# GpSimd's weight splitting placed behind the first layernorm's operations, two per-row scalars, and the dummy matmuls of the steady state taken out

## What is computed

```
x = x + linear_attention(layernorm(x))         # 16 heads of 16, feature elu(.)+1, own wq wk wv wo and biases
x = x + cross_attention(layernorm(x), ctx)     # 16 query heads, 4 key/value heads, ALiBi bias, mask, softmax
x = x + moe(layernorm(x))                      # 8 experts of 176, top 2, plus a shared expert of 352
layernorm(x) = (x - mean) / sqrt(var + 1e-5)
```

## Time and profile before

| | |
|---|---|
| three runs | 467.52, 468.42, 465.21 us; median 467.52 |
| profiled execution | 467.31 us, span of its instructions 465.5 us |
| mean granted TensorE clock | 0.957 |
| busy PE, DVE, ACT, POOL | 393.8, 299.8, 222.8, 216.4 us |
| attention pipeline | to about 270 us, the expert stage to 465.5 us |

### The profile page before, as it was taken

The page is one execution under the profiler, slowest core; times in us unless marked ns, Lnnn a source line. Parts: engine busy times, 40 slices in busy tenths (PEclk is TensorE's granted clock), DMA queues, the critical chain, the costliest instruction groups (busy, mean ns, idle before and its releaser), DMA issues.

```text
span 465.5 us, 12494 instructions
## 1 busy us (share of the span) xinstructions
PE 393.8 (85%) x4014; PEld 329.3 (71%) x4014; DVE 299.8 (64%) x808; ACT 222.8 (48%) x576; POOL 216.4 (46%) x252
## 2 busy tenths in 40 slices
PE   7888899888988899889997868999999999998300
PEld 5666667666776667667776757999988999887200
DVE  2636877778667877788764268666666566655166
ACT  2224356544664356544544274788445555544200
POOL 1135567565766567665554200777214444333300
PEclk9989999999999999999999997999999999999755
DMA  7910213151141420500000000223323333332396
GB/s 183 328 64 13 57 46 104 56 147 46 18 140 55 129 58 14 145 11 0 13 1 2 2 0 1 103 102 107 97 59 115 114 114 114 113 95 89 98 283 218
DMA packets 30583, 40.21 MB, mean 86 GB/s; under 512 B 6354, under 2 KB 23634, under 8 KB 30546
## 3 DMA queue, kind: packets, MB, share of 16 engines
q1 hardware_dynamic: 24210, 27.56, 20.9%
q0 software_dynamic: 3456, 9.46, 5.7%
q10 hardware_dynamic: 2880, 2.69, 1.8%
HBM read 22.88 MB, written 16.81 MB: 85 GB/s over the span
## 4 chain that ended last, share of the span: by engine, by line
PE 52%; DVE 18%; issue 12%; DMA 7%; ACT 2%; POOL 2%; DVEq 1%; POOLq 0%; SPq 0%; ACTq 0%
PE ps L761 22%; PE ps L524 5%; DVE smax L1252 4%; PE ps L640 4%; DMA y_rows<-e_y,out_row 4%; PE ps L627 3%; DMA yg<-y_rows 3%; PE ps L602 3%; PE ps L533 2%; PE ps L571 2%; PE ps L856 2%; DVE xn L1239 2%; PE ps L841 2%; DVE kv_bd L1202 1%; PE ps L515 1%
## 5 line engine op out<-in xcount | busy, mean ns | idle before, releaser
L495 POOL DMA_INDIRECT y_rows<-e_y,out_row x40 | 38.4, 959 | 69.6 <-ACT e_y L1110 32.7
L761 PE MATMUL ps<-w_hi,xh 128*128 (+1 forms) x144 | 49.8, 346 | 9.4 <-DVE xl L1363 5.8
L436 POOL TENSOR_TENSOR sc<-sc,smax 128x1024 f32<-128x1024 f32 x16 | 32.7, 2041 | 43.3 <-DVE smax L1252 43.3
L761 PE MATMUL ps<-w_hi,xl 128*128 (+1 forms) x144 | 47.3, 328 | 0.0
L761 PE MATMUL ps<-w_lo,xh 128*128 (+1 forms) x144 | 47.0, 327 | 0.0
L487 POOL DMA_INDIRECT xs_rows<-x_send,pos x32 | 30.9, 966 | 29.8 <-DVE pos L1462 20.4
L681 PE MATMUL ps<-zeros 128*128 128x256 f32 x142 | 40.2, 416 | 4.2 <-DVE key_off L1297 2.9
L429 POOL TENSOR_TENSOR bias_t<-alibi,key_off 128x1024 f32<-128x1024 f32 x16 | 37.8, 2364 | 0.0
L761 PEld LDWEIGHTS ps<-w_hi,xh 128*128 128x128 f32 x144 | 27.4, 190 | 13.6 <-issue 6.4
L402 POOL TENSOR_TENSOR st<-mv,eps 128x1 f32<-128x1 f32 x32 | 6.1, 190 | 59.9 <-DVE mv L1164 30.7
L681 PEld LDWEIGHTS ps<-zeros 128*128 128x128 f32 x142 | 26.4, 201 | 7.9 <-issue 3.1
(11 more groups left out here) (178 smaller groups left out, 1143.8 us busy)
## 6 DMA issues: line engine op xcount, KB each, us to landing
w_stage<-in_w_ffn_dram SPq DMA_DIRECT2D x12, 496.0 KB, 3.8
xs_rows<-zeros SPq DMA_DIRECT2D x5, 1028.0 KB, 7.3
xs<-xs_rows SPq DMA_DIRECT2D x40, 128.5 KB, 2.1
yg<-y_rows SPq DMA_DIRECT2D x16, 256.0 KB, 3.8
ctxT<-in_ctxT_dram SPq DMA_DIRECT2D x16, 128.0 KB, 2.1
out_dram<-y ACTq DMA_DIRECT2D x16, 128.0 KB, 3.8
x_all<-in_x_dram SPq DMA_DIRECT2D x1, 1664.0 KB, 9.8
y_rows<-e_y,out_row POOLq DMA_INDIRECT x40, 2.9
```

Source lines behind the costliest of these rows:

```text
L436: nc.gpsimd.tensor_tensor(v, v, spread(smax[:, :].rearrange("p (h o) -> p h o", o=1), 2, S), ALU.subtract).then_inc(sm["sub_ready"], 1)
L495: nc.gpsimd.indirect_dma_start(out=y_d[:, :], out_offset=bass.IndirectOffsetOnAxis(ap=out_row[:, q:q + 1], axis=0), in_=e_y[:, q, :], in_o ...
L761: mm = T.matmul(out_ap, lhs, rhs[rows, cols], start=st, stop=en)
```

## The change

Three edits. On POOL `rstd1(t+2)` is issued before `split_low` and no longer behind it. On DVE `xn1` and `xn2` are tensor_scalars: one tensor, and two scalars per row. On PE the two zero matmuls in `transpose_x2` (t = 0 to 14) and the single one in `transpose_o2` (tiles 0 to 13) are gone; the other dummy matmuls stay.

```diff
                 if has(t, 0):
                     rstd2(t)
+                if has(t, 2):
+                    rstd1(t + 2)
                 if splits(t):
                     split_low(t - FIRST_SPLIT, q)
-                if has(t, 2):
-                    rstd1(t + 2)
...
             def transpose_x2(t):
                 pe.wait_ge(sm["q1_ready"], 2 * (t + 2 if has(t, 1) else t + 1))
-                if has(t, 1):
-                    keep_warm(A0, 2)
                 pe.wait_ge(sm["ln2_done"], t + 1)
...
             def transpose_o2(t):
-                if has(t, 2):
-                    T.matmul(ps[:, B0, 2 * P:4 * P], zeros[:, 0:P], zeros[:, 0:D], start=True, stop=True)
                 pe.wait_ge(sm["o2_ready"], t + 1)
...
             def ln1_norm(t):
-                V.scalar_tensor_tensor(out=xn1[:, :], in0=xt(t), scalar=mv1[:, 0:1], in1=spread(rs1[:, :], 1, D),
-                                       op0=ALU.subtract, op1=ALU.mult).then_inc(sm["ln1_done"], 1)
+                V.tensor_scalar(xn1[:, :], xt(t), mv1[:, 0:1], rs1[:, :], ALU.subtract, ALU.mult).then_inc(sm["ln1_done"], 1)
...
             def ln2_norm(t):
-                V.scalar_tensor_tensor(out=xn2[:, :], in0=xt(t), scalar=mv2[:, 0:1], in1=spread(rs2[:, :], 1, D),
-                                       op0=ALU.subtract, op1=ALU.mult).then_inc(sm["ln2_done"], 1)
+                V.tensor_scalar(xn2[:, :], xt(t), mv2[:, 0:1], rs2[:, :], ALU.subtract, ALU.mult).then_inc(sm["ln2_done"], 1)
```

## The result

The changed kernel takes 445.11 us, the median of four runs (442.98, 446.16, 447.91, 444.06). The kernel before took 467.97 us beside it (four runs, 465.21 to 469.15). The ratio is 0.9523 with a 95% interval of 0.9451 to 0.9595, so it is faster by 4.8%. The forecast was 441.5 us in a range of 437.5 to 449.5. The profiled execution is the fastest of the four: 442.98 us, 24.3 us under the profiled 467.31 of before.

What follows compares the result with a forecast made beforehand. It took a 15.01 us loop through PE and DVE, with xn2 stalled by POOL's split, as the bound: 467.31 - 23.2 - 2.8 - 0.7 + 0.6 = 441.2, plus 0.3 for the clock, gives 441.5 us. Range 437.5 to 449.5.

Steps and rivals of the forecast that it cites:

- Exclusion of DVE and POOL: In the loop, a DVE operation with two SBUF inputs waits for a running POOL operation; xn2 took 2.40 us for 0.48.
- doesn't do it: Rival: xn2 stalls for another reason than POOL's split, so the time stays at 464 to 468 us; chance 0.02.
- The split behind `rstd1`: On POOL in t = 2 to 13: moving the split removes xn2's stall, 1.93 us an iteration, 23.2 us over twelve.
- The collision with `xn1`: On DVE, xn1 meets the last 0.10 us of the moved split; 0.05 us an iteration, 0.6 us in all.
- Two per-row scalars: On DVE, xn1 and xn2 take 0.36 us each, saving 0.12 each time: 2.8 us in the loop, 0.7 before it.
- The clock at the start: In t = 0 and 1, fewer PE records before gaps could bring a second low-clock stretch: 0.3 us, ends 0 and 1.5.
- The dummies: PE's zero matmuls cost nothing before the change; kept after it, the pair would hide 1.1 us of gain each time.
- PE's own loop: PE's iteration without its waits and the zero matmuls: 12.54 us, 0.30 under the new loop of 12.84.
- PE becomes the bound: Rival: PE or a hidden chain sets the loop, costing 0.3 to 1.0 us an iteration, 445 to 454 us; chance 0.15.
- POOL's subtraction goes first: Rival: the split ends late and xn1 waits for all of subtract_max, 2.07 us an iteration, 465 us; chance 0.06.
- The clock falls in the loop: Rival: without dummies PE loses full clock, 8.8 us per wholly low iteration, 494 us with six; chance 0.03.

Runs made afterwards that it cites:

- order_back: The kernel after with POOL's split ahead of rstd1 again, scalars per row and no dummies kept: 486.36 us for 483.49 before, ratio 1.0065.
- split_later: The kernel after with an unused POOL addition of zeros ahead of the split, so that it ends later: 469.22 us for 483.33 before, ratio 0.9724.
- order_only: The kernel before with only rstd1 moved ahead of the split on POOL: 444.13 us for 466.13 before, ratio 0.9522.
- dummies_back: The kernel after with all the removed dummy matmuls put back: 461.50 us for 483.49 before, ratio 0.9535.
- warm_start: The kernel after with a pair of zero products ahead of transpose_x2 in t = 0 and 1 only: 456.43 us for 483.49 before, ratio 0.9429.
- no_dummies_only: The kernel before with only the dummy matmuls taken out: 489.12 us for 483.33 before, ratio 1.0119.
- stt_back: The kernel after with the old two-tensor form of xn1 and xn2: 461.53 us for 483.49 before, ratio 0.9526.
- warm_gaps: The kernel after with zero products: a pair in t = 0 and 1, six at the start of t = 1, three behind its transpose_x2; ratios 0.9428 and 0.9419.

## Why the prediction was right, and where its steps were not

The sign, the mechanism and the range were right: 445.11 lies in 437.5 to 449.5. It is 3.6 us above the 441.5. The profiled execution is only 1.5 us above it, and that is in part luck, as the last sum shows. Step by step:

1. **Exclusion of DVE and POOL: right.** `xn2` took 2.28 to 2.43 us in the twelve iterations and takes 0.40, and came back to 2.25 when only the order was undone (`order_back`). The change that "doesn't do it" is excluded. The prediction left open whether the new form is held too: it is.

2. **The split behind `rstd1`: right in place and size.** Start 0.91 us after the score addition (0.90 predicted), end 3.21 after it (3.19). The stall of 1.93 us an iteration is gone. The collision with `xn1` was booked at 0.05 us and costs nothing: a held tensor_scalar ends 0.15 us after POOL's operation, which is 185.50 us here, and `xn1` ends at 185.63 anyway. A longer collision costs, as the 0.43 us of `split_later` show (122.98 for 122.55). The weight loads, started later, stay hidden: ACT's `split_high` waits for nothing in the loop.

3. **Two per-row scalars: right in kind, too large.** The estimate was 0.36 us, from the 0.29 of L1339 and 0.07 for a scalar; it is 0.40, with 0.31 or 0.32 to the next start in place of 0.27. An operation saves 0.07 us and not 0.12. The loop by the measured terms is 15.01 - 2.00 (stall and `xn2`, 2.32 to 0.32) - 0.07 (`xn1`) = 12.94 us, for 12.95 in the trace and 12.84 forecast. Over twelve iterations that is 1.3 us of the error. Before t = 2 the 0.7 us booked were too much as well: `order_only` and `dummies_back` differ by this edit alone, and take 15.43 and 15.29 us in t = 0, 12.67 and 12.53 in t = 1, so 0.28 us of it are shown.

4. **The clock at the start: the term of the sum that was mis-sized most.** I booked 0.3 us within ends of 0 and 1.5, from the earlier trace rows. Measured were +2.19 us in t = 1 of the profiled execution, outside those ends, and 0.87 and 0.93 in two others. I had seen the danger ("four records less before such gaps in t = 0 and 1") and priced it by one short operation, L588. But the low stretch lasts from 39 to 45 us and takes in `project_q2` and all that follows it. `warm_start` shows the cause: two pairs of zeros put back in t = 0 and 1 bring t = 1 to 12.53 us.

5. **The dummies: "cost nothing as the kernel stands" held for the waits, not for the clock.** PE did idle behind them. But they also held the clock under the stall: `no_dummies_only` is 1.2% slower. The third edit depends on the first: the prediction saw this for the waits, and not for the clock. The other half, that 1.1 us an iteration would stay hidden with them in place, was too large by four times: 0.26 us. Three readings of the earlier trace rows went wrong. I took L657's duration of 1.03 us for the time until the next operation starts, which is 0.86 in `order_only` (157.90 to 158.76). And I kept L580 at its old place behind the pair, though it had been waiting there for `xn2`: it starts 0.97 us after the pair does in `order_only` (156.71 to 157.68) and 1.21 after it in the earlier trace rows. And I gave the single product ahead of L651 0.03 us of PE's own loop, though it takes 0.54 from its start to the next where PE doesn't wait (155.12 to 155.66). So PE's own loop is that of `order_only`, in which it never waits, without the zeros: 13.24 - 0.97 - 0.54 = 11.73 us, and not 12.54. The mean loop of 12.98 us had 1.25 us of room (the brackets show only 0.80, since they count from the modelled ends). Of the 1.51 us of zeros this takes up all but 0.26, which is what they cost.

6. **The rivals.** *PE becomes the bound*: not in the kernel after, where PE's own loop leaves 1.25 us of room and not the 0.30 that the rival was priced on; with the dummies it does, at 13.24 us. *POOL's subtraction goes first*: excluded by `split_later`. *The clock falls in the loop*: it did not in the kernel after (1.00 from 50 to 206 us, PE at 94%, 93% predicted), but it does in `no_dummies_only` and `order_back`, where the stall is there and the dummies are not. It was a real mechanism whose condition was missing here, rather than an unlikely one.

**The sum with measured terms**, profile against profile: 25.4 us were forecast for the twelve iterations (12 x 2.12) and 24.5 came (1.95 + 11 x 2.05); 0.7 for the operations before t = 2 and 0.6 came (0.45 + 0.18), of which the 0.45 is not shown to be the change's; the clock was to take 0.3 and took 2.2; and 1.5 us came out of the expert stage, booked at nothing. This is 24.4 us for 25.8. Without the 1.5 and the 0.45, which nothing ties to the change and which I count as luck, the profile would stand at 444.9 us (467.31 - 22.4), 3.4 above the forecast. The four runs spread from 442.98 to 447.91, and their median lies 2.1 us above the profiled one.

**What each edit is worth.** By the ratios, `order_only` 0.9522, `dummies_back` 0.9535, `stt_back` 0.9526 and the full change 0.9517 to 0.9545 can't be told apart. By the loop, in which more can be seen, the first edit gives 15.03 to 13.24 us; on top of it the third alone gives 13.13, the second alone nothing (13.24), both 12.98. Without the first edit no run has the second alone; `order_back`, which has it with the third, keeps the stall. What both give, some 3 us over twelve iterations, is partly handed back at once by the low clock of t = 1 (0.9 to 2.2 us). `warm_start` and `warm_gaps` keep the loop of 12.98 us, lose the low stretch, and reach 0.942 to 0.943; from the first `xn2` to the last they are 2.6 to 3.9 us shorter than the three profiles of the kernel after.

## What to carry to other kernels

When an operation on VectorE takes five times its usual duration, lay GpSimd's timeline beside it before calling it slow. If it ends just behind one of GpSimd's large operations, try to move GpSimd's operation into a stretch where VectorE reads PSUM or reduces one tensor: here that was worth the whole stall, and rewriting VectorE's as a tensor_scalar did not lift it. Judge products of zeros last and gap by gap: those in a loop that no longer has gaps can go, those in the first iterations, where the engine still waits for loads and constants, should stay, and it is worth trying to add to them. And where a chain is shortened, take each operation's cost as the time to the next start, from rows in which the engine doesn't wait, and ask of each operation on the other engine whether it stood where it stood for a reason that the change removes.

## What was not expected of the hardware

- A GpSimd operation on SBUF tensors held VectorE's scalar_tensor_tensor with two SBUF tensors for its whole length, and a tensor_scalar with a single one as well (2.25 us for 0.40). The tensor_scalar ends 0.15 us after GpSimd's operation, the scalar_tensor_tensor of the earlier trace rows 0.29 us after it. A collision of 0.12 us cost nothing.
- A 128x256 fp32 tensor_scalar with two operations and two scalars per row takes 0.40 us, 0.11 more than the one of the earlier trace rows, which has one operation with a constant. What part the scalars have in it was not separated.
- The clock's fall after an idle gap is not the same in every execution: after 2.79 us without work it fell in one profile and not in another of the same work.
- The chips differ. The kernel before takes 483 us on two and 466 to 467 on two others. The kernel after shows where, in its groups by line from 270 to 440 us (count, busy us and mean ns, idle time before), first on the chip with 460.55 us, then on the one with 443.07:

```profile
L487 POOL DMA_INDIRECT xs_rows<-x_send,pos x30 | 28.9, 962 | 24.0 <-ACT x_send L951 17.3 <-issue 6.7
```

```profile
L487 POOL DMA_INDIRECT xs_rows<-x_send,pos x30 | 28.8, 961 | 9.1 <-issue 8.5 <-ACT x_send L951 0.6
```

The attention stage takes 196.03 us from the first to the last `xn2` on both. The 18.4 us between the two profiled spans lie in the expert stage, where the scattering of rows waits 24.0 us for 9.1; why it does on that chip, no run here shows.
